# A fused block of three layers on one core: VectorE's order in the window attention of layer one, and output products of the feed-forward issued inside its loop

## The reference, cut to what matters

```python
def _get_graph_features(feats, inds_list, perm, W_lin, b_lin, k=K):
    ...
    scores = jnp.einsum('bihd,bjhd->bhij', qh, qh) / np.float32(np.sqrt(headdim))
    attn = jax.nn.softmax(scores, axis=-1)
    out = jnp.einsum('bhij,bjhd->bihd', attn, qh).reshape(B * N, k, total)
```

```python
def _qlora_linear(x, wq, A, B):
    w = jnp.tile(wq, (1, 4))
    base = x @ w.T
    lora = x @ A.T @ B.T
    return base + lora * LORA_SCALING
gate = jax.nn.silu(_qlora_linear(x, w1q, a1, b1))
up = _qlora_linear(x, w3q, a3, b3)
return _qlora_linear(gate * up, w2q, a2, b2)
```

## Time and profile before

| what | us |
|---|---|
| median of 3 runs | 2203.59 |
| lowest and highest | 2200.35, 3210.74 |
| the profiled execution | 2203.48 |
| its span, first to last instruction | 2201.7 |
| VectorE busy | 1840.4 (84%) |
| TensorE busy | 1865.4 (85%) |
| ScalarE busy | 1596.5 (73%) |
| GpSimd busy | 1071.2 (49%) |

### The profile page before, as it was taken

How to read it: one execution, slowest core, us unless ns; L and a number is a source line. 1 busy time by engine, 2 the same in 40 slices (tenths; PEclk the granted TensorE clock), 3 DMA queues, 4 the chain that set the end, 5 groups by cost and what they waited for, 6 DMA issues and landing times. The chain is left out here.

```text
span 2201.7 us, 99587 instructions
## 1 busy us (share of the span) xinstructions
PE 1865.4 (85%) x37653; PEld 1274.8 (58%) x37656; DVE 1840.4 (84%) x3511; ACT 1596.5 (73%) x3296; POOL 1071.2 (49%) x1160
## 2 busy tenths in 40 slices
PE   4876688888885674899999994879999999999957
PEld 2333377777773333899999993424545554554522
DVE  8899889999995996799999996847888888888864
ACT  7899778888886996899999993565554554454432
POOL 1220189999992002687788771003445444544511
PEclk9976699999996666999999996999999999999977
DMA  1157865555551776545545531302222222222110
GB/s 37 37 122 175 187 140 126 121 120 127 119 110 34 177 175 159 108 105 110 108 105 108 110 83 45 92 27 91 82 86 76 81 86 79 83 81 86 48 51 20
DMA packets 434897, 215.53 MB, mean 98 GB/s; under 512 B 301196, under 2 KB 404268, under 8 KB 434681
## 3 DMA queue, kind: packets, MB, share of 16 engines
q1 hardware_dynamic: 431872, 212.24, 40.0%
q10 hardware_dynamic: 2936, 2.18, 0.4%
HBM read 161.35 MB, written 52.86 MB: 97 GB/s over the span
## 5 line engine op out<-in xcount | busy, mean ns | idle before, releaser
L1015 PE MATMUL pQ<-QM,QX 128*128 128x96 f16 x2880 | 299.6, 227 | 1.6 <-issue 1.6
L1013 PE MATMUL pQ<-neigh_lo,QX 128*128 128x64 f16 x2880 | 292.7, 195 | 3.3 <-issue 3.3
L1013 PEld LDWEIGHTS pQ<-neigh_lo,QX 128*128 128x128 f16 x2880 | 276.3, 103 | 3.1 <-issue 3.1
L1015 PEld LDWEIGHTS pQ<-QM,QX 128*128 128x128 f16 x2880 | 274.8, 103 | 2.1 <-issue 2.1
L2656 POOL TENSOR_TENSOR MT<-cb,decay 128x512 f32 (+1 forms) x128 | 174.8, 1386 | 207.7 <-DVE half L2567 152.5
L1571 PE MATMUL pQ<-QM,QX 128*128 128x64 f16 x2880 | 232.0, 206 | 0.0
L1569 PE MATMUL pQ<-neigh_lo,QX 128*128 128x32 f16 x2880 | 227.5, 182 | 0.0
L1569 PEld LDWEIGHTS pQ<-neigh_lo,QX 128*128 128x128 f16 x2880 | 218.9, 103 | 2.8
L1111 POOL TENSOR_TENSOR Dm<-Sc,mx 128x450 f32<-128x450 f32 x192 | 183.1, 954 | 71.5 <-DVE mx L1071 71.5
L1571 PEld LDWEIGHTS pQ<-QM,QX 128*128 128x128 f16 x2880 | 212.4, 104 | 0.3
L1435 POOL TENSOR_TENSOR QT<-QT,R 128x450 f32<-128x450 f32 x192 | 183.0, 953 | 37.1 <-DVE R L1503 28.2
(11 more groups left out here) (455 smaller groups left out, 5221.9 us busy)
## 6 DMA issues: line engine op xcount, KB each, us to landing
QM<-scratch_q SPq DMA_DIRECT2D x192, 240.0 KB, 2.7
QX<-scratch_q SPq DMA_DIRECT2D x768, 60.0 KB, 2.3
scratch_q<-QT SPq DMA_DIRECT2D x124, 360.0 KB, 5.1
Wo<-in_out_proj SPq DMA_DIRECT2D x64, 256.0 KB, 2.6
Wg<-in_in_proj SPq DMA_DIRECT2D x62, 256.0 KB, 2.7
Wh<-in_in_proj SPq DMA_DIRECT2D x62, 256.0 KB, 2.8
W_s<-in_in_proj SPq DMA_DIRECT2D x20, 256.0 KB, 2.7
CT<-scratch_c SPq DMA_DIRECT2D x192, 11.2 KB, 2.1
```

The source lines that it names most:

```text
L1013: nc.tensor.matmul(pQ[:, p, u // PB, o + 32:o + BW], qx[u], W["neigh_lo"][:, 0:O], start=False, stop=True, skip_group_check=True)
L1015: last = nc.tensor.matmul(pQ[:, p, u // PB, o:o + BW], qx[u], qm[u], start=False, stop=True, skip_group_check=True)
```

## The change

In `windows_and_attention`, VectorE's step is reordered. Before: maximum (k - 1), sum (k - 3), transpose (k - 4), reciprocal (k - 3). After: sum (k - 3), maximum (k - 1), reciprocal (k - 3), transpose (k - 4). The maximum over neighbours stays last. Layer two's attention keeps its order.

In `feed_forward`, the output products of the first two thirds r of the inner rows are issued early. A new function `piece(q, r)` issues three of them. Five pieces go into tiles 7 to 11 of the loop, between `adapters(n)` and `low_rank(n - 1)`; three follow behind the loop, ahead of `low_rank(11)`. Only the last third and the f32 product stay in the final loop over q. The outputs lie in the banks `pt[:, 0]`, `pt[:, 1]`, a new bank `pr`, and `pg[:, 0]`. So that the operands are there in time, the split of W2 moves from tile 5 to tile 3 and the splits of `uf` from tiles 7 and 11 to tiles 5 and 9.

```diff
             def step(k, at):
+                if at(3):
+                    (t, _), p = at(3), (k - 3) % ND
+                    dve.wait_ge(exped, t + 1 + ND)
+                    v.tensor_reduce(Z[:, p, :], valid(E[:, p, :]), X, ALU.add).then_inc(summed, 1)
                 if at(1):
...
                 if at(3):
                     (t, _), p = at(3), (k - 3) % ND
-                    dve.wait_ge(exped, t + 1 + ND)
-                    v.tensor_reduce(Z[:, p, :], valid(E[:, p, :]), X, ALU.add).then_inc(summed, 1)
+                    dve.wait_ge(summed, t + 1)
+                    v.reciprocal(R[:, p, :], Z[:, p, :]).then_inc(r_ready, 1)
                 if at(4):
...
                     v.transpose(AT[:, k5 % NA, :], A[:, k5 % ND, :]).then_inc(turned, 1)
-                if at(3):
-                    (t, _), p = at(3), (k - 3) % ND
-                    dve.wait_ge(summed, t + 1)
-                    v.reciprocal(R[:, p, :], Z[:, p, :]).then_inc(r_ready, 1)
...
+        EARLY = {7: (0, 0), 8: (1, 0), 9: (2, 0), 10: (0, 1), 11: (1, 1)}
...
+        pr = ctx.enter_context(nc.psum_tensor("pr_f", [128, 512], F32))
...
+        def out_of(q):
+
+            return (pt[:, 0, :], pt[:, 1, :], pr[:, :], pg[:, 0, :])[q]
...
-                if n % 4 == 3 and n >= 4:
+                if n % 4 == 1 and n >= 4:
                     act.wait_ge(uf_ready, 3 * (n // 4))
...
-                if n == 5:
+                if n == 3:
                     v.scalar_tensor_tensor(W2[:, 1, :, :], w2[:, :, :], UP, W2[:, 0, :, :], ALU.mult, ALU.subtract)\
                         .then_inc(w2_split, 1)
-                if n % 4 == 3 and n >= 4:
+                if n % 4 == 1 and n >= 4:
                     r = n // 4 - 1
...
+            def piece(q, r):
+
+                pe.wait_ge(uf_split, r + 1)
+                for a, b in ((0, 0), (0, 1), (1, 0)):
+                    nc.tensor.matmul(out_of(q), uf16[:, a, r, q * 128:(q + 1) * 128], W2[:, b, r, :],
+                                     start=r + a + b == 0, stop=False)
...
                 adapters(n)
+                if n == 7:
+                    pe.wait_ge(w2_split, 1)
+                if n in EARLY:
+                    piece(*EARLY[n])
                 low_rank(n - 1)
+            piece(2, 1)
+            pe.wait_ge(u_ready, HT - 1)
+            piece(3, 0)
+            piece(3, 1)
             low_rank(HT - 1)
-            pe.wait_ge(w2_split, 1)
-            pe.wait_ge(la2_ready, 1)
-            pe.wait_ge(uf_split, FR)
             for q in range(TT):
-                po = (pg if q < 2 else pu)[:, q % 2, :]
-                for r in range(FR):
-                    for a, b in ((0, 0), (0, 1), (1, 0)):
-                        nc.tensor.matmul(po, uf16[:, a, r, q * 128:(q + 1) * 128], W2[:, b, r, :],
-                                         start=r + a + b == 0, stop=False)
+                piece(q, FR - 1)
+                if q == 0:
+                    pe.wait_ge(la2_ready, 1)
+                po = out_of(q)
                 nc.tensor.matmul(po, la2[:, q * 128:(q + 1) * 128], b2[:, :], start=False, stop=True).then_inc(out_mm, 1)
```

More of the change, by code:

```diff
@@ L2906, in _ @@
                 dve.wait_ge(out_mm, q + 1)
-                v.scalar_tensor_tensor(res[:, q, :], (pg if q < 2 else pu)[:, q % 2, :], 1.0 / UP, x2[:, q, :],
+                v.scalar_tensor_tensor(res[:, q, :], out_of(q), 1.0 / UP, x2[:, q, :],
                                        ALU.mult, ALU.add).then_inc(res_ready, 1)
```

## The result

The changed kernel takes 2175.56 us (median of 7 runs, 2171.52 to 2179.97), before 2201.1 beside it: ratio 0.9887, 95% interval 0.9865 to 0.9908, 25 us less. Timed once more on another occasion (experiment 8) the ratio is 0.9919 (0.9894 to 0.9943), 18 us less. The profiled execution has a span of 2170.7 us. One execution of before of 3210.74 us stands alone and is left out.

What follows compares the result with a forecast made beforehand. Engines waiting for each other in a ring bound layer one's attention; the feed-forward's end was a chain of waits, then a low-clock tail. 2203.5 - 10 (attention) - 14 (tail) = 2179.5, say 2180 us; range 2166 to 2195.

Steps and rivals of the forecast that it cites:

- The ring of 1.97 us and its cut: Layer one's attention: reciprocal, product, transpose, reciprocal close at 1.97 us a step; the reciprocal ahead of the transpose cuts this.
- The new ring of 3.76 over two steps, four steps at 8.00: Layer one's attention: maximum, subtraction, product, transpose, sum take 3.76 us; two such plus 0.48 make 8.00, against 8.23.
- Attention 10 us: Layer one's attention, 9 us from the steps and 1 from the drain: -10 us, from -3 to -17.
- The sum's wait costs nothing: Layer one's attention: VectorE's sum, now first, has 0.8 us of slack behind ScalarE's exponential, so its wait costs nothing.
- The loop +1.8, the tail's last part 1.2 later: Feed-forward: loop 1.8 us longer (+0.5 to +3), tail's head 0.6 shorter, so the products' last part starts 1.2 later.
- The tail, 14 us: Feed-forward's last output products: fewer matmuls, full clock for the first two thirds; 14 us saved after the later start.
- The clock: TensorE in the tail: enters at full clock from dense pieces, held for two thirds, since the f16 and f32 mixture returns.
- (a): Rival: the tail keeps the full clock to its end; 15.6 + 10 us gained, 2178 us; chance 0.15.
- (b): Rival: the tail's clock falls at once; 9.7 + 10 us gained, 2184 us; chance 0.12.
- (c): Rival: attention's links are longer in the new order, so it gains nothing; 2189.5 us, 2193.5 with (b); chance 0.17.
- (d): Rival: attention's ring is looser, four steps go to VectorE's own 7.48 us; 36 + 14 gained, 2153 us; chance 0.06.
- (e): Rival, slower: attention's sum waits for an exponential queued on ScalarE; 56 us more, 2246 us with part two; chance 0.03.

Runs made afterwards that it cites:

- experiments 4 and 5: Before with one VectorE edit in layer one's attention: reciprocal ahead of transpose, maximum still first (ratio 0.9943); or sum first, reciprocal still behind transpose (1.0021).
- hmax_mid: Changed kernel with the maximum over neighbours one step later, between reciprocal and transpose in layer one's attention; 2166.79 us, ratio to before 0.9864.
- ord_mzrt: Before with VectorE's order maximum, sum, reciprocal, transpose in layer one's attention; ratio to before 0.9943, 12 us less.
- after_again: The changed kernel, unaltered, timed and profiled once more beside before; 2179.01 us against 2197.16, ratio 0.9919.
- before_again: The kernel of before, unchanged, profiled and timed once more; ratio to itself 0.9992, profiled execution 2190.6 us.
- later: Changed kernel with no piece in tile 10: piece (0, 1) goes to tile 11 and (1, 1) behind the loop; ratio to before 0.9921.
- best: Changed kernel with the maximum over neighbours between reciprocal and transpose, and tile 10 without a piece; 2169.26 us, ratio to before 0.9873.
- both_layers: Changed kernel with VectorE's new order in layer two's attention as well; ratio to before 0.9935.
- Experiment 6: Before with fourteen unread f16 matmuls added, nine ahead of low_rank(11) and five behind it; ratio to before 0.9974, 5 us less.
- the parts: Before with only the attention's diff (2183.48 us, ratio 0.9948), and before with only the feed-forward's diff (2187.66 us, ratio 0.9962).

## Why the prediction was right, and where it was not

The whole was 24 us forecast, 25 and 18 measured, inside the range both times. By its steps:

- **The ring of 1.97 us and its cut.** Right. The product's wait for the reciprocal is gone, and experiments 4 and 5 show that the reciprocal's place alone did it. The sum of the old ring was 0.09 short because it took each transpose 0.03 behind its product: once in four steps it is 0.14, and that step takes 2.07 (transposes at 449.75 and 451.82) and not 1.97.
- **The new ring of 3.76 over two steps, four steps at 8.00.** Four steps take 8.00 in the changed kernel, with two waiting transposes of four as said, and `hmax_mid` shows the bound by filling the wait. That it comes out to the hundredth is in part luck. From maximum to maximum the first ring takes 3.69 (450.07 to 453.76), not 3.76, and the second, with the maximum over neighbours in it, 4.31 (to 458.07), not 4.24. Nor is the ring alone. GpSimd waits for a maximum by more than some hundredths only once in four steps (43 waits in 350 us); that subtraction and the next three operations follow each other at 0.91 (450.76 to 453.48), the second waiting transpose stands behind the last of them, and the rest up to the maximum of 458.07 is VectorE's own queue. That path is as long as the two rings, within some hundredths. That VectorE's own work allowed 7.48 was wrong for this order: without its two waits (0.19 and 0.15) it would take 7.66, and the four steps of `ord_mzrt` stand at 8.02 with no wait for GpSimd.
- **Attention 10 us.** Right: 11 (7 to 16), and 8 to 11 by the spans of the maxima (396.3 and 394.7 before, 385.7 and 386.6 after). The drain gave 0.8 where I had put 1.
- **The sum's wait costs nothing.** Right: no wait of `Z` for ScalarE is in the list.
- **The loop +1.8, the tail's last part 1.2 later.** Right: passes(0) to passes(11) take 37.1 in `after_again` and 35.3 in `before_again`, and `la2` comes 1.4 later. I had put 0.6 to 1.1 on the half moved to tile 9, and it costs 0.9 there. A tile with a piece takes 3.00, a little over my floor of 2.90.
- **The tail, 14 us.** This is the term that was mis-sized. The step said "from the same point it is 22.8 now", as if the low clock belonged to the kernel. It belonged to one execution: the same kernel has a tail of 14.1 us in another. Measured, the part is worth 8 us (5 to 12), and 5 against the short tail. That the changed kernel's tail starts at the full clock and loses it on the way was right; only the last block falls in five of the eight profiles that have this tail, the last two in `later`, `best` and `both_layers`.
- **The clock.** Experiment 6 is on the side of the Trainium skill's rule (TensorE: Matmul & The Clock Gate, Part 1), that activity releases the low clock: entered busy, the old tail stays at 1.00 for 12.5 us. My argument against it, that 21 us of unbroken work at 0.50 show the mixture to be at fault, fell. Yet in the changed kernel, with three f16 matmuls between the f32 pairs and not nine, the clock does fall in the last block or two, in unbroken work, in all eight profiles. What of the mixture decides stays open.
- **The rivals.** (a), the full clock throughout, did not happen, (b) and (c) neither; (d) and (e) are excluded by 8.00 and by the missing wait.

That the total came out at the first comparison's 25 owed something to luck: the parts say 20, and the second comparison says 18.

## What to carry to other kernels

When engines at 85 to 95% wait for each other, write the ring down link by link from the starts in the timeline; it says which instruction's place matters, and about how long the next ring will be: 3.69 here where 3.76 was summed. Look also for a second path of the same length, such as one engine's operations back to back. Then put work that nobody in the ring waits for into the place where the ring waits. Before a stage with a low granted clock enters a sum as the kernel's own, look whether a second execution has it too: here a 9 us difference in one stage came and went with the same program.

## What the runs showed of the hardware

TensorE's clock came back in three different ways at the same work: in the first profile of before it stayed at 0.50 through 21 us of back-to-back products, in the second it was at 1.0 after the first block of nine, and entered from dense work it never fell. The eight f32 products ahead of the loop took 6.54 us at 0.50 (`before`), 3.60 at 1.00 (`after`) and 5.00 with a change on the way (`before_again`, `after_again`), in kernels that are the same there.

A transpose on VectorE of 128 x 480 has no single cost. From its start to the next one's it takes 0.54 to 0.55 where it followed its reciprocal at once and a sum or the maximum of a tile stands behind it (450.75 to 451.30 in the changed kernel, 450.82 to 451.37 in experiment 4), and 0.60 to 0.61 where it had waited, with a sum behind it (452.66 to 453.26) as with a reciprocal (453.78 to 454.39).
